# A four-place ring for the first layer's expert weights, filled at the first and second scatter of the following expert

## The chip, the cores and the metric

The kernel runs on one core of one Trainium2 chip. The metric is the device time of one execution in microseconds, as the median of several runs.

## The reference, cut to what matters

A graph network of two layers on 1250 nodes with 512 features. Each layer adds a message-passing part and an attention part to its input and then a mixture of experts. The change touches the experts of the first layer alone:

```python
# first layer, on x = layernorm(...), 1250 x 512
gate_probs = softmax(x @ gate_w.T)                 # 16 experts
top_v, top_i = top_k(gate_probs, 4); top_v = softmax(top_v)
for e in range(16):
    routed += combine[:, e:e+1] * (gelu(x @ re_w1[e] + re_b1[e]) @ re_w2[e] + re_b2[e])   # 512 -> 256 -> 512
shared = mean of two experts that every node goes through
x = x + routed + shared
```

The second layer has 16 experts of another form (two of 16 for a node, 512 to 768 to 512, gated). All arithmetic is in float32.

## The kernel before, in words

The program is a sequence of stages, each a block in which SP (SyncE, which asks for the plain transfers), POOL (GpSimd), PE (TensorE), ACT (ScalarE) and DVE (VectorE) run their own streams and meet at the end. `stage_experts` (line 1084) calls two of them for each layer. `stage_front` computes the gate and the two shared experts, ranks the nodes of each expert (`find_places`) and writes one row for each node to the tensor `token_rows` in HBM. `stage_routed` (line 2012) then goes through the routed experts.

`stage_routed` works in tiles of 128 rows. The rows of one expert fill whole tiles, so an expert has two to four tiles here, and there are 48 tiles in the first layer. For tile g:

- POOL gathers the 128 rows of a tile by an indirect DMA (line 2110, from `token_rows`, two tiles ahead of their use);
- PE turns them (line 2178), DVE copies them (2325, 2326), PE multiplies by the expert's w1 (2194), DVE adds b1 (2332), ACT applies the gelu (2288), PE turns the result (2204), ACT copies it (2280), and PE multiplies by w2 (2214);
- ACT scales the result by the rows' weights (`weigh`, line 2294), and POOL adds it to the rows of `token_sums` in HBM by an accumulating indirect DMA (`add_rows`, line 2119). This is called the scatter of the tile below.

POOL does its part in the order of `tile` (line 2123): copy the scatter's row numbers (`know_add`, 2102) once the scatter two tiles before has landed, since that scatter used the same buffers; issue a gather (2110); wait for the gather before it and copy the next gather's row numbers (2098); wait for earlier scatters; issue the scatter (2119). ACT's `weigh` of a tile waits for `know_add` of it. Two experts can send results to the same node, and an accumulating write is not safe against another to the same row. So the scatter of an expert's first tile waits until all scatters of earlier experts have landed (`landed_by`, lines 2124 and 2138). Scatters of one expert touch different rows and may overlap.

**The ring.** The weights of an expert (w1 512 KB, b1 spread over 128 partitions 128 KB, w2 512 KB) lie in one place of a ring of `RING_EXPERTS` = 3 places at the end of the on-chip arena. Expert e has place e mod 3 (counted from the end). `load_expert` (line 1037) asks for them on SP's queue: w1 (line 1044) and b1 (1045), then w2 (1049). `stage_front` loads the first `early` = 3 experts. In `stage_routed` SP goes through e = 3 to 15 (line 2073): it waits until PE has finished the last w2 product of expert e-3, whose place this is (`down_ready`, which counts PE's tiles; `done_by` holds the number of tiles up to and with an expert, plus one), asks for w1 and b1, then waits until POOL has begun the scatter of the first tile of expert e-2 (`add_begun`, counted just ahead of each scatter), and asks for w2. After the weights of experts 7, 9, 11 and 13 it also asks for 1 MB each of the next stage's attention weights (`MIX_AT`; line 378).

In the second layer the ring has 3 places too, and w2 has no wait of its own.

`find_places` (line 1396, on DVE) derives the place of each tile's expert, `ring_of`, by taking the number of places off again and again, in 5 rounds of two linked operations (lines 1444 to 1448).

Of the kernel before, what the change touches and what calls it, by code (L numbers as in the profile page):

```python
# [25 lines left out]
P = 128  # L26
NODES = 1250
TS = 125
NT = NODES // TS
D = 512  # L30
# [19 lines left out]
ROW = D + NE  # L50
RING_EXPERTS = 3
AHEAD = 4
# [963 lines left out]
class L0_EXPERTS:  # L1016

    top, shared, shared_weight, swiglu = 4, 2, 0.5, False
    slots, early = P, 3
    ff, blocks, w1_cols = 256, 2, 256  # L1020
# [5 lines left out]
class L1_EXPERTS:  # L1026

    top, shared, shared_weight, swiglu = 2, 1, 1.0, True
    slots, early = P, 1
    ff, blocks, w1_cols = 384, 3, 768  # L1030
# [6 lines left out]
def load_expert(sp, rt, kind, ins, e, between=lambda: None):  # L1037

    if e:
        sp.wait_ge(rt.w1_loaded, 32 * e)
    w1, w2, b1 = rt.slot_parts(rt.ring[:, RING_EXPERTS - 1 - e % RING_EXPERTS, :])
    sp.dma_start(w1, ins[kind.w1][e].rearrange("(k p) n -> p k n", p=P)).then_inc(rt.w1_loaded, 16)  # L1044
    sp.dma_start(b1, ins[kind.b1][e].unsqueeze(0).to_broadcast([P, kind.w1_cols])).then_inc(rt.w1_loaded, 16)
    if e:
        sp.wait_ge(rt.w2_loaded, 16 * e)
    between()
    sp.dma_start(w2, ins[kind.w2][e].rearrange("(f p) n -> p f n", p=P)).then_inc(rt.w2_loaded, 16)
# [34 lines left out]
def stage_experts(nc, st, ar, kind, ins, kept, fi, out=None, mw=None, free=None):  # L1084
# [8 lines left out]
    SLOT = KT * W + F * D + W  # L1093
    rt.ring = ar.whole[:, ar.end - RING_EXPERTS * SLOT:ar.end].rearrange("p (r n) -> p r n", r=RING_EXPERTS)
    rt.slot_parts = lambda slot: (slot[:, 0:KT * W].rearrange("p (k n) -> p k n", k=KT),
# [24 lines left out]

    stage_routed(nc, st, SplitArena(ar.whole, free or [(DYN, DYN + KT * NODES + NT * D), (ar.at, ar.end - RING_EXPERTS * SLOT)]),
                 kind, ins, rt, out, mw)


def stage_front(nc, st, ar, kind, ins, rt, fi):
# [62 lines left out]
    with ExitStack() as ctx:  # L1188
# [207 lines left out]
        def find_places(dve):  # L1396
# [46 lines left out]
            link(dve.tensor_copy(rt.expert_of, expert_f))  # L1443
            for r in range(RING_EXPERTS, NE, RING_EXPERTS):
                link(dve.tensor_scalar(lap, expert_f, RING_EXPERTS - 0.5, -float(RING_EXPERTS), ALU.is_gt, ALU.mult))
                link(dve.tensor_tensor(expert_f, expert_f, lap, ALU.add))
            link(dve.tensor_scalar(expert_f, expert_f, -1.0, RING_EXPERTS - 1.0, ALU.mult, ALU.add))
            link(dve.tensor_copy(rt.ring_of, expert_f))
# [563 lines left out]
def stage_routed(nc, st, ar, kind, ins, rt, out, mw):  # L2012
# [4 lines left out]
    F, W, SW = kind.blocks, kind.w1_cols, kind.swiglu  # L2017
    R = RING_EXPERTS
    TILES = 2 * rt.most_pairs
# [23 lines left out]
    with ExitStack() as ctx:  # L2043
# [27 lines left out]
        @block.sync  # L2071
        def _(sp):
            for e in range(kind.early, NE):
                if e >= R:
                    done = sp.value_load(rt.done_by[0:1, e - R:e - R + 1], min_val=1, max_val=TILES + 1)
                    sp.wait_ge(down_ready, done)
                if e >= R and not SW:

                    load_expert(sp, rt, kind, ins, e, lambda: sp.wait_ge(add_begun, done))
                else:  # L2080
                    load_expert(sp, rt, kind, ins, e)
                if mw is not None and e in MIX_AT:
                    mw.load(sp, MIX_AT[e])
            sp.wait_ge(w1_loaded, 32 * NE)
            sp.wait_ge(w2_loaded, 16 * NE)
            sp.wait_ge(all_added, 1)
            if out is None:
                for h, (t0, t1) in enumerate(HALVES):
                    load_tiles(sp, st.res3, sums[1:NODES + 1, :], t0, t1, sums_read[h])
                sp.wait_ge(sums_read[0], 32)  # L2090
                sp.wait_ge(sums_read[1], 32)
# [412 lines left out]
```

## Time and profile before

| | |
|---|---|
| median of 3 runs | 2342.08 us (2335.74, 2342.08, 2342.43) |
| the profiled execution's own time | 2335.63 us |
| its span | 2333.8 us |
| granted TensorE clock, mean | 0.979 |
| PE busy | 2161.1 us, 93% of the span |
| DVE, ACT, POOL busy | 1004.2, 507.6, 309.7 us |
| first to last scatter of the first layer | 842.0 to 1072.3 us, 48 scatters |

Times in the trace are microseconds from the span's start. The span is the time from the first to the last instruction. The profiled execution is the one from which all rows below come. A row of the timeline gives start, duration, engine, line, operation and operands, and in square brackets the idle time of the engine ahead of it with what ended that time. SPq rows are requests for transfers: their duration is that of the request, not of the transfer. An indirect DMA on POOL has the time POOL needs to issue it; the transfer goes on after it. The scatters are numbered here from 0, as they come: scatter 0 is at 842.01.

### The profile page before, as it was taken

What the parts mean: (1) busy time and instruction counts of PE and PEld (TensorE: products, weight loads), DVE (VectorE), ACT (ScalarE), POOL (GpSimd) and SP (SyncE); (2) the same over time, 40 slices, a digit from 0 to 9 for tenths busy, and PEclk for the clock granted to TensorE, in tenths of its full rate; (3) what the DMA queues carried; (4) which work ended last, traced back from release to release, by engine and by line L of the source; (5) the groups of instructions that cost most, each with busy time, mean ns of one, the idle gap of its engine ahead of it and who ended that gap; (6) DMA issues with size and microseconds to landing.
All of it is one profiled execution on the core that took longest, in us unless ns stands there. A gap on an engine that the chain in (4) does not pass through costs nothing. (4 is left out here: it accounts for less than half of the span.)

```text
span 2333.8 us, 26804 instructions
## 1 busy us (share of the span) xinstructions
PE 2161.1 (93%) x7344; PEld 1242.2 (53%) x7345; DVE 1004.2 (43%) x2731; ACT 507.6 (22%) x903; POOL 309.7 (13%) x393
## 2 busy tenths in 40 slices
PE   6998889999998989885999999999899999989997
PEld 3444444545355445554544378854488854545553
DVE  7966778401114622222043465412265413634443
ACT  2112131110103012223111154211244212201221
POOL 1200000000000046562300000000000010013443
PEclk9999999999999999998999999999999999999998
DMA  4003000000002258885000000010100002248773
GB/s 127 1 0 119 1 1 18 1 18 0 0 0 96 90 121 201 222 197 104 36 0 27 25 12 1 1 63 0 37 1 1 1 5 70 80 154 269 216 240 95
DMA packets 77202, 154.58 MB, mean 66 GB/s; under 512 B 10217, under 2 KB 21524, under 8 KB 77116
## 3 DMA queue, kind: packets, MB, share of 16 engines
q1 hardware_dynamic: 59452, 113.06, 14.7%
q0 software_dynamic: 17664, 40.43, 8.7%
q8 instruction: 47, 0.77, 0.1%
q14 instruction: 39, 0.32, 0.0%
HBM read 119.50 MB, written 36.18 MB: 67 GB/s over the span
## 5 line engine op out<-in xcount | busy, mean ns | idle before, releaser
L1918 PE MATMUL bank<-arena 125*125 125x257 f32 x1600 | 355.8, 383 | 4.8 <-DVE arena L1837 4.8
L1918 PEld LDWEIGHTS bank<-arena 125*125 125x125 f32 x1600 | 302.2, 189 | 60.5 <-DVE arena L1837 6.4
L2194 PE MATMUL bank<-arena 128*128 x832 | 258.9, 446 | 13.4 <-issue 6.6
L973 PE MATMUL bank<-arena 125*128 125x500 f32 (+1 forms) x720 | 253.5, 513 | 3.1 <-ACT arena L1002 2.3
L473 PE MATMUL bank<-arena 128*125 128x512 f32 x480 | 212.6, 592 | 2.2 <-PEq L319 2.2
L2194 PEld LDWEIGHTS bank<-arena 128*128 128x128 f32 x832 | 152.0, 193 | 109.7 <-issue 60.0
L1712 PE MATMUL bank<-arena 128*125 128x512 f32 x480 | 207.8, 593 | 1.0 <-PEq L409 1.0
L973 PEld LDWEIGHTS bank<-arena 125*128 125x128 f32 x720 | 135.5, 189 | 121.1 <-issue 109.7
L2214 PE MATMUL bank<-arena 128*128 x360 | 171.2, 604 | 6.2 <-ACT arena L2280 4.0
L2332 DVE TENSOR_TENSOR arena<-bank,arena 128x384 f32<-128x384 f32 (+1 forms) x104 | 51.7, 497 | 257.1 <-PE bank L2194 211.6
L1896 ACT ACTIVATE arena<-arena 125x625 f32<-125x625 f32 x160 | 134.5, 900 | 102.4 <-DVE arena L1837 102.2
L1712 PEld LDWEIGHTS bank<-arena 128*125 128x125 f32 x480 | 89.4, 188 | 113.0 <-issue 112.8
L473 PEld LDWEIGHTS bank<-arena 128*125 128x125 f32 x480 | 86.7, 187 | 101.2 <-issue 101.2
L1837 DVE SCALAR_TENSOR_TENSOR arena<-arena 125x625 f32<-125x625 f32 x160 | 132.4, 864 | 15.6 <-ACT arena L1896 15.6
L735 DVE TENSOR_SCALAR arena<-arena 125x500 bf16<-125x500 f16 x432 | 117.2, 345 | 36.5 <-PE bank L777 36.3
L1768 DVE CUSTOM_DVE_ANT_0 arena<-arena 125x256 f32<-125x256 f32 x160 | 58.2, 422 | 161.5 <-ACT arena L1755 134.7
L913 DVE TENSOR_TENSOR arena<-bank,arena 128x500 f32<-128x500 f32 (+1 forms) x36 | 21.3, 592 | 244.1 <-PE bank L973 244.1
L777 PE MATMUL bank<-arena 125*125 125x500 bf16 x432 | 106.8, 381 | 18.3 <-DVE arena L735 18.2
L2110 POOL DMA_INDIRECT arena<-token_rows,arena x76 | 80.1, 1053 | 163.9 <-DVE arena L2326 129.4
L2214 PEld LDWEIGHTS bank<-arena 128*128 128x128 f32 x360 | 61.6, 191 | 63.0 <-issue 62.0
L777 PEld LDWEIGHTS bank<-arena 125*125 x432 | 57.9, 135 | 69.3 <-issue 52.7
L960 PE MATMUL bank<-arena 128*125 128x512 f32 x184 | 84.0, 619 | 10.5 <-DVE arena L891 9.4
(336 smaller groups left out, 2277.4 us busy)
## 6 DMA issues: line engine op xcount, KB each, us to landing
arena<-in_L_ffn_expert_w SPq DMA_DIRECT2D x16, 1536.0 KB
arena<-in_L_ffn_re_w SPq DMA_DIRECT2D x32, 512.0 KB
arena<-in_L_ffn_expert_w SPq DMA_DIRECT2D x16, 768.0 KB
arena<-in_L_mix_Wqkv SPq DMA_DIRECT2D x6, 1024.0 KB, 10.8
arena<-in_L_gnn_W SPq DMA_DIRECT2D x3, 2048.0 KB, 8.1
arena<-in_L_ffn_expert_b SPq DMA_DIRECT2D x16, 384.0 KB
token_rows<-arena SPq DMA_DIRECT2D x2, 2500.0 KB
arena<-in_L_gnn_W SPq DMA_DIRECT2D x3, 1024.0 KB, 5.5
```

The lines of the kernel that those rows point to most:

```text
L473: last = pe.matmul(st.bank[n % 4][0:TS, :], st.turned[:, k, t * TS:(t + 1) * TS], w3[:, k, j * D:(j + 1) * D], start=(k == 0), stop=(k == ...
L735: last = dve.tensor_scalar(marks[:, u, :], st.iota16[:, 0:WIN * NT], float(w * WIN * NT), keys[:, u:u + 1], ALU.add, ALU.is_equal)
L777: last = pe.matmul(bank, stays[:, u, :], marks[:, u, :], start=False, stop=False, skip_group_check=True)
L960: last = pe.matmul(st.bank[s % 4][0:TS, :], X[:, k, s * TS:(s + 1) * TS], w[:, k, :], start=(k == 0), stop=(k == KT - 1))
L973: last = pe.matmul(st.bank[4 + n % 4][:, 0:cn], h[s][:, f * P:(f + 1) * P], st.counts[:, s, c0:c0 + cn], start=(s == 0), stop=(s == NT - 1))
L1712: last = pe.matmul(st.bank[n % 4][0:TS, :], x, w[:, half * 512:(half + 1) * 512], start=(k == 0), stop=(k == K - 1))
L1837: dve.scalar_tensor_tensor(out=prob[:, u % 2, s, :], in0=excess[:, n % EXCESS, :], scalar=by_one[:, s, head:head + 1], in1=st.counts16[:, ...
L1896: act.activation(excess[:, n % EXCESS, :], row[:, head, d0:d0 + HALF], ACT.Relu, scale=by_fifth[:, s, head:head + 1], bias=minus_one[:, s, ...
L1918: return pe.matmul(st.bank[n % OUTS][0:TS, 0:ONCOL], prob[:, u % 2, s, j * TS:(j + 1) * TS], st.slots[:, head + 1, s, :], start=(s == 0), ...
L2110: pool.indirect_dma_start(out=rows[b], out_offset=None, in_=rt.table, in_offset=bass.IndirectOffsetOnAxis(ap=get_row[b].bitcast(mybir.dt.u ...
L2194: last = pe.matmul(st.bank[UP[b][h]][:, 0:WP], xt[b][:, k, :], rt.ring[:, bass.ds(r, 1), k * W + h * WP:k * W + (h + 1) * WP].rearrange("p ...
L2214: last = pe.matmul(st.bank[DOWN[b]], ht[b][:, f, :], rt.ring[:, bass.ds(r, 1), W2_AT + f * D:W2_AT + (f + 1) * D].rearrange("p a n -> p (a ...
```

## The change

The number of places becomes a property of the layer: 4 in the first, 3 in the second. In the first layer SP's wait for a place changes with it. Expert e now takes the place of expert e-4. w1 and b1 are asked for when POOL has begun the scatter of the first tile of expert e-3, the one that follows the place's owner, and w2 at the scatter after that. The second layer's rule stays (`down_ready`). The four attention loads still follow the w2 request of their expert.

```diff
-RING_EXPERTS = 3
 ...
 class L0_EXPERTS:
-    slots, early = P, 3
+    slots, early, ring = P, 3, 4
 class L1_EXPERTS:
-    slots, early = P, 1
+    slots, early, ring = P, 1, 3
 ...
 def load_expert(sp, rt, kind, ins, e, between=lambda: None):
-    w1, w2, b1 = rt.slot_parts(rt.ring[:, RING_EXPERTS - 1 - e % RING_EXPERTS, :])
+    w1, w2, b1 = rt.slot_parts(rt.ring[:, kind.ring - 1 - e % kind.ring, :])
 ...
-            for r in range(RING_EXPERTS, NE, RING_EXPERTS):
-                link(dve.tensor_scalar(lap, expert_f, RING_EXPERTS - 0.5, -float(RING_EXPERTS), ALU.is_gt, ALU.mult))
+            for r in range(kind.ring, NE, kind.ring):
+                link(dve.tensor_scalar(lap, expert_f, kind.ring - 0.5, -float(kind.ring), ALU.is_gt, ALU.mult))
                 link(dve.tensor_tensor(expert_f, expert_f, lap, ALU.add))
 ...
-    R = RING_EXPERTS
+    R = kind.ring
 ...
             for e in range(kind.early, NE):
                 if e >= R:
                     done = sp.value_load(rt.done_by[0:1, e - R:e - R + 1], min_val=1, max_val=TILES + 1)
-                    sp.wait_ge(down_ready, done)
+                    sp.wait_ge(down_ready if SW else add_begun, done)
                 if e >= R and not SW:
-                    load_expert(sp, rt, kind, ins, e, lambda: sp.wait_ge(add_begun, done))
+                    load_expert(sp, rt, kind, ins, e, lambda: sp.wait_ge(add_begun, done + 1))
                 else:
                     load_expert(sp, rt, kind, ins, e)
```

How the instructions stand on the engines is shown at two places. A name in a bracket is that of a semaphore; semaphores are reused, so `step_49` is here `down_ready` and `ident_ready_49` is `add_begun`. `re_w` stands for w1 (line 1044, in the changed kernel 1043) and w2 (1049, then 1048), `re_b` for b1.

SP before, at the start of `stage_routed` of the first layer: the loads of experts 3 and 4.

```order
L2071 UNCONDITIONAL_BRANCH [waits barrier_Pool_Activation_PE_DVE_SP_release]
L2075 TENSOR_LOAD arena
L2075 ISA x2
L1044 DMA arena<-in_L_ffn_re_w 128x4x256 [waits w1_loaded_4,step_49]
L1045 DMA arena<-in_L_ffn_re_b 128x256
L1049 DMA arena<-in_L_ffn_re_w 128x2x512 [waits ident_ready_49,w2_loaded_4]
L2075 TENSOR_LOAD arena
L2075 ISA x2
L1044 DMA arena<-in_L_ffn_re_w 128x4x256 [waits w1_loaded_4,step_49]
L1045 DMA arena<-in_L_ffn_re_b 128x256
L1049 DMA arena<-in_L_ffn_re_w 128x2x512 [waits ident_ready_49,w2_loaded_4]
```

SP with the change, at the same place.

```order
L2070 UNCONDITIONAL_BRANCH [waits barrier_Pool_Activation_PE_DVE_SP_release]
L1043 DMA arena<-in_L_ffn_re_w 128x4x256 [waits w1_loaded_4]
L1044 DMA arena<-in_L_ffn_re_b 128x256
L1048 DMA arena<-in_L_ffn_re_w 128x2x512 [waits w2_loaded_4]
L2074 TENSOR_LOAD arena
L2074 ISA x2
L1043 DMA arena<-in_L_ffn_re_w 128x4x256 [waits w1_loaded_4,ident_ready_49]
L1044 DMA arena<-in_L_ffn_re_b 128x256
L2079 REGISTER_ALU [waits w2_loaded_4]
L1048 DMA arena<-in_L_ffn_re_w 128x2x512 [waits ident_ready_49]
```

Expert 3 is loaded at once, with no wait for a tile; from expert 4 on both parts wait for scatters, and neither for PE.

DVE in `find_places` with the change (first layer). Before, lines 1445 and 1446 (now 1444 and 1445) stood there five times each.

```order
L1442 CAST arena<-arena 125x56
L1444 TENSOR_SCALAR arena<-arena 125x56
L1445 TENSOR_TENSOR arena<-arena 125x56
L1444 TENSOR_SCALAR arena<-arena 125x56
L1445 TENSOR_TENSOR arena<-arena 125x56
L1444 TENSOR_SCALAR arena<-arena 125x56
L1445 TENSOR_TENSOR arena<-arena 125x56
L1446 TENSOR_SCALAR arena<-arena 125x56
```

Two of five rounds are gone, four operations in all.

## Rows read from the trace of the kernel before

**Rows 1.** Line 2119 in the window 842 to 1075: count, issue time, first and last start.

```profile
L2119 POOL DMA_INDIRECT token_sums<-arena x48: 1591/1598/1626, 842.0 to 1072.3; - x48
```

**Rows 2.** Stretches: width, busy PE, PEld, DVE, ACT, POOL; clock, DMA share, GB/s.

```profile
920.00:1027.00 107.00, 95.08 (x382) 56.37 (x381) 25.03 (x64) 29.99 (x64) 62.90 (x84) 1.00 0.89 222
...
1037.00:1065.00 28.00, 26.24 (x106) 16.02 (x106) 6.32 (x16) 8.75 (x18) 17.99 (x24) 1.00 0.73 130
```

**Rows 3.** Timeline of POOL, scatters 3, 12, 13, 14, 15 and 16, and one copy.

```profile
858.93 1.60 POOL L2119 DMA_INDIRECT token_sums<-arena  x1 [1.42 <-DMA token_sums<-arena]
...
899.56 1.60 POOL L2119 DMA_INDIRECT token_sums<-arena  x1 [0.53 <-issue]
906.70 1.60 POOL L2119 DMA_INDIRECT token_sums<-arena  x1 [1.81 <-DMA token_sums<-arena]
...
910.25 1.60 POOL L2119 DMA_INDIRECT token_sums<-arena  x1 [0.31 <-issue]
911.79 0.26 POOL L2102 COPY arena<-arena 128x1 int32 x1
...
914.35 1.60 POOL L2119 DMA_INDIRECT token_sums<-arena  x1 [0.44 <-issue]
...
920.26 1.60 POOL L2119 DMA_INDIRECT token_sums<-arena  x1 [1.09 <-issue]
```

**Rows 4.** The same timeline: a copy and the scatters 18, 19, 25, 31.

```profile
928.87 0.18 POOL L2102 COPY arena<-arena 128x1 int32 x1 [3.18 <-DMA token_sums<-arena]
...
931.03 1.60 POOL L2119 DMA_INDIRECT token_sums<-arena  x1 [0.17 <-issue]
...
936.63 1.60 POOL L2119 DMA_INDIRECT token_sums<-arena  x1 [2.17 <-DMA token_sums<-arena]
...
966.47 1.60 POOL L2119 DMA_INDIRECT token_sums<-arena  x1 [2.19 <-DMA token_sums<-arena]
...
996.79 1.60 POOL L2119 DMA_INDIRECT token_sums<-arena  x1 [2.23 <-DMA token_sums<-arena]
```

**Rows 5.** The same timeline: scatter 37, a copy, scatters 39 and 45.

```profile
1027.13 1.60 POOL L2119 DMA_INDIRECT token_sums<-arena  x1 [2.17 <-DMA token_sums<-arena]
...
1033.21 0.23 POOL L2102 COPY arena<-arena 128x1 int32 x1
...
1037.50 1.60 POOL L2119 DMA_INDIRECT token_sums<-arena  x1 [1.93 <-DMA token_sums<-arena]
...
1065.09 1.60 POOL L2119 DMA_INDIRECT token_sums<-arena  x1 [1.61 <-DMA token_sums<-arena]
```

**Rows 6.** Timeline of SP's requests around scatters 13 to 16, and by scatter 37.

```profile
906.00 0.37 SPq L1049 DMA_DIRECT2D arena<-in_L_ffn_re_w  x1
911.91 0.37 SPq L1044 DMA_DIRECT2D arena<-in_L_ffn_re_w  x1
...
919.57 0.37 SPq L1049 DMA_DIRECT2D arena<-in_L_ffn_re_w  x1
919.98 0.46 SPq L378 DMA_DIRECT2D arena<-in_L_mix_Wqkv  x1
...
1028.32 0.37 SPq L1044 DMA_DIRECT2D arena<-in_L_ffn_re_w  x1
```

**Rows 7.** Waits in the window 842 to 1072: who for whom, us, times, longest.

```profile
PE bank L2214 <- DMA arena<-in_L_ffn_re_w: 1.0, 2, 0.7
```

**Rows 8.** The attention weights' three loads 920 to 980, time to landing.

```profile
DMA to landing us min/median/max: 7.1/8.1/8.4
```

**Rows 9.** Timelines: the start of `stage_routed`, POOL's gather and PE's second turn.

```profile
829.45 0.98 POOL L2145 DMA_INDIRECT arena<-token_rows,arena  x1 [0.57 <-POOL arena L2142]
...
837.97 0.60 PE L2178 MATMUL bank<-arena 128*128 128x128 f32 x4
```

**Rows 10.** Timelines of DVE and PE in `stage_front`: a ring round, the wait behind.

```profile
786.62 0.22 DVE L1446 TENSOR_TENSOR arena<-arena 125x56 f32<-125x56 f32 x1
...
795.89 3.68 PE L1332 MATMUL bank<-arena 128*125 128x512 f32 x8 [0.17 <-DVE arena L1600]
```

More of the change, by code:

```diff
@@ L1093, in stage_experts @@
     SLOT = KT * W + F * D + W
-    rt.ring = ar.whole[:, ar.end - RING_EXPERTS * SLOT:ar.end].rearrange("p (r n) -> p r n", r=RING_EXPERTS)
+    rt.ring = ar.whole[:, ar.end - kind.ring * SLOT:ar.end].rearrange("p (r n) -> p r n", r=kind.ring)
     rt.slot_parts = lambda slot: (slot[:, 0:KT * W].rearrange("p (k n) -> p k n", k=KT),
@@ L1119, in stage_experts @@
     stage_front(nc, st, Arena(ar.whole, ar.at, ar.end - kind.early * SLOT), kind, ins, rt, fi)
-    stage_routed(nc, st, SplitArena(ar.whole, free or [(DYN, DYN + KT * NODES + NT * D), (ar.at, ar.end - RING_EXPERTS * SLOT)]),
+    stage_routed(nc, st, SplitArena(ar.whole, free or [(DYN, DYN + KT * NODES + NT * D), (ar.at, ar.end - kind.ring * SLOT)]),
                  kind, ins, rt, out, mw)
@@ L1443, in find_places @@
             link(dve.tensor_copy(rt.expert_of, expert_f))
-            for r in range(RING_EXPERTS, NE, RING_EXPERTS):
-                link(dve.tensor_scalar(lap, expert_f, RING_EXPERTS - 0.5, -float(RING_EXPERTS), ALU.is_gt, ALU.mult))
+            for r in range(kind.ring, NE, kind.ring):
+                link(dve.tensor_scalar(lap, expert_f, kind.ring - 0.5, -float(kind.ring), ALU.is_gt, ALU.mult))
                 link(dve.tensor_tensor(expert_f, expert_f, lap, ALU.add))
-            link(dve.tensor_scalar(expert_f, expert_f, -1.0, RING_EXPERTS - 1.0, ALU.mult, ALU.add))
+            link(dve.tensor_scalar(expert_f, expert_f, -1.0, kind.ring - 1.0, ALU.mult, ALU.add))
             link(dve.tensor_copy(rt.ring_of, expert_f))
```

## The prediction

> **What bounds the kernel now.** The change touches one stage, the routed experts of the first layer, so I went from the page to the stretch in which this stage's scatters run: 48 of them, from 842.0 to 1072.3 [rows 1]. The table of stretches comes first. While weights are loaded (920 to 1027) PE is busy for 95.08 of 107 us (89%), and the DMA engines for 0.89 of the time; once nearly all are in (1037 to 1065), PE is busy for 26.24 of 28 us (94%) and the DMA share is 0.73 [rows 2]. PE does not wait for the weights themselves: its products with w2 stand behind that weight's transfer for 1.0 us in the whole stage [rows 7]. So something that the weight traffic slows stands between.
>
> The timeline of POOL shows what. Take three experts: tiles 10 to 12, 13 to 15, and 16 to 18. The first tile's scatter of an expert must find all earlier scatters landed, and it does wait: scatter 13 comes 7.14 us after scatter 12, scatter 16 comes 5.91 after 15, scatter 19 comes 5.60 after 18 [rows 3, 4]. I call this time the **boundary**. The other half of the period is the time from an expert's first to its last scatter, the **inside**. There the last tile's row copy has to wait for the first tile's scatter to land, since both use the same buffers: scatter 15 comes 7.65 after 13, but scatter 18 comes 10.77 after 16 [rows 3, 4]. So a period holds two landings in series, that of the first tile's scatter and that of the last tile's. The middle tile's landing is not in this chain unless it is over 2 us late. In a stretch with almost no loads, six tiles take 27.59 us, 13.8 for three [rows 5]; with loads and attention weights six tiles take 29.93 (13 to 19), 29.84 (19 to 25), 30.32 (25 to 31) and 30.34 (31 to 37) [rows 3 to 5].
>
> SP's rows say which load stands beside which landing. A w2 is asked for 0.70 us before an expert's first scatter (906.00, 919.57), a w1 with its b1 2.44 us before its last (911.91 before 914.35), and 1 MB of attention weights 0.28 us before a first scatter (919.98) [rows 3, 6]. The two bad cases follow. Where w1 stands beside the last scatter, the boundary is 5.91 to 7.14 us, against 5.60 with none (18 to 19). Where the attention weights stand beside the first scatter, its landing is late and the copy behind it comes at 928.87, 8.61 us after the scatter; without them it comes at 911.79, 5.09 us after [rows 3, 4].
>
> **The change, part by part.** Times are of the profiled execution, 2335.63 us, whose span is 2333.8.
>
> *w1 leaves the last scatter.* After the change w1 goes out 0.7 us before an expert's first scatter, w2 0.7 before its second, and nothing near the last one. So a boundary should be 5.60.
>
> *w1 stands beside the first scatter.* There w2 stood before, and the copy came 5.09 us later, when POOL was free for it, so w2 cost nothing there. How w1 with b1 does is not seen alone. Lower bound: as w2, nothing. Upper bound: scatter 37, which has a w2 (0.70 before) and a w1 (asked for at 1028.32, 1.19 after) beside it; its copy comes after 6.08 us, 1.0 later than the 5.09 [rows 5, 6]. w1 with b1 is 640 KB against 1152 KB there and 512 KB of w2, so I take nearer to the lower end: 0.4. The inside becomes 8.05, a period without attention weights 8.05 + 5.60 = 13.65. The stretch almost without loads ran at 13.8, part of it limited by PE's own pace; I take 13.7.
>
> Ten tiles, scatters 3 to 13, took 47.77 [rows 3]. At 13.7 for three tiles they take 45.7, and the four-tile expert among them has only one boundary for four tiles, some 0.5 less: 45.2. **Gain 2.6.**
>
> *The attention weights move.* They follow a w2, so they now go out right ahead of a middle scatter. Its late landing is off the chain: the middle comes 3.6 after the first (906.70 to 910.25), its copy 8.6 later, and a next first scatter 2.2 behind the copy (928.87 to 931.03), which is 14.4, less than the period below. What they still do is slow the last scatter, 4.5 us behind. Lower bound: nothing, a boundary of 5.60. Upper bound: w2, attention weights and the w1 ahead of them fill the DMA engines past the last scatter; the worst boundary in rows 3 and 4 is 7.14, and I put the bound at 8.0 (estimate). I take 7.0, near the 7.14 that a w1 beside the last scatter gave. The period is 8.05 + 7.0 = 15.05, and with its partner without attention weights 13.7 + 15.05 = 28.75. Four such pairs take 115.0, against 120.43 from scatter 13 to 37 [rows 3, 5]. **Gain 5.4.**
>
> *The ends.* Scatters 37 to 39 (10.37 us) have w1 and w2 beside them before and after; from 39 on there is next to nothing: 0. At the start, expert 3 is now loaded at once (1152 KB), beside the first gathers; the one issued at 829.45 is turned by PE at 837.97, and 8 us cover a delay of a few [rows 9]. If that cover were gone the cost would be 1 to 2 us. The w1 that stood beside the first tiles goes, and there scatters wait for one another anyway: 0.
>
> *DVE.* Four linked operations of 0.22 us, some 0.9 us, go from `stage_front`. PE waits behind them only 0.17 [rows 10], so **0.2** at most.
>
> *SP and PE.* SP's queue is idle between requests, and an added register instruction costs nothing there. Weights arrive three tiles sooner; with PE's waits for w2 at 1.0 us in all [rows 7] (and those I read as the last of several causes), I count 0. The second layer is as before.
>
> Sum: 2.6 + 5.4 + 0.2 = 8.2 us, so 2327.4 for the profiled execution. The median of the three runs is 2342.08, 6.4 above it, so the prediction is **2333.9**. What comes next as the bound is PE, at the pace of the last stretch.
>
> The Trainium skill ("DMA: Bandwidth & Descriptors", section "Queues, rings and completion order") says that a transfer's completion count is written only after every earlier write of that DMA engine, across its queues. It speaks against this change, since w1 would then hold the first scatter's landing until its own data is down; the trace agrees as far as that with 1 MB ahead, which takes 8.1 us to land [rows 8], the scatter's copy comes 8.61 us later. By it the sum would be that of the first rival.
>
> **Rivals.**
>
> 1. *The burden only changes place.* The first scatter lands only when w1 and b1 have, some 6 us after it is begun, as with scatter 37 (6.08) [rows 5]. Each inside grows by 1.0, not 0.4. For it: the mix-laden scatter's landing follows that of the 1 MB. Against it: w2 in the same place costs nothing. Price: 0.6 more in about 11 periods, 6.6 of the 8.2 go back: 2340.5, no difference. The point: a copy 6 us after the first scatter.
>
> 2. *Slower: the two sets pile up.* w1 and w2 are now 3.6 us apart and not 5.9 or 7.7 [rows 3, 6]. If the engines are not done with one when the next and two gathers come, first and last scatter are late together. The DMA share is already 0.89 [rows 2]. Price: a copy after 7.0 us, between 6.08 and the 8.61 of the mix, makes the inside 9.6, a period 15.2, and one with attention weights 9.6 + 7.0 = 16.6. Ten tiles take 15.2 x 10/3 = 50.7 (2.9 lost), four pairs 127.2 (6.8 lost): 9.7 slower, 2351.8. It decides from where an average period of 14.3 (47.77 x 3/10) is passed: a copy later than 6.2 us. Against it: nothing is then asked for from the second scatter to the next first, which lets the engines catch up.
>
> 3. *It does not do what it says.* SP asks in order, and each request also waits until the previous expert's has landed. Were that late, w1 would slip from the first scatter to a later one. Against it: before, w2 went out at 906.00 and the next w1 at 911.91, with time between [rows 6]. Then about 2342.
>
> **How the numbers follow.** My forecast has 0.62, rival 1 has 0.21, rival 2 0.12, rival 3 0.05. The measurement can tell about 0.3%, 7.0 us. The forecast's own bounds: at best 8.2 + 0.4 x 11 + 1.4 x 4 = 18.2, but the last stretch's pace (27.59 / 6 = 4.60 a tile) leaves 13.0 (scatters 3 to 39: 36 tiles at 4.60 are 165.6, against 178.6), so 13 and 1 for a PE a little faster still; at worst 8.2 - 0.6 x 11 - 1.0 x 4, 2.4 slower. Within it 0.44 lies beyond 7.0 and 0.18 inside. Rival 1 gives 0.19 to no change and 0.02 to slower, rival 2 its 0.12 to slower, rival 3 its 0.05 to no change. Together 0.44, 0.42, 0.14. The runs before lie at 2335.74 and at 2342, so the lower end is 2335.7 less 14, and the upper end 2342.4 plus 3.5.
>
> **What would show it.** Right: w1 0.7 us before each first scatter from scatter 3 on; boundaries of 5.6 in all experts without attention weights; insides of about 8; pairs at 28.75; the time from scatter 3 to 39 some 8 us under 178.6. Wrong: row copies of last tiles more than 6 us after the first scatter, boundaries of over 7 with nothing beside them, or PE waiting for gathers with the chain of scatters already short.

## The result, and the profile after

The change makes the kernel slower, by 0.6%: 2352.94 us median (2349.47 to 2354.31, 4 runs) against 2340.63 (2335.74 to 2342.43, 4 runs); ratio 1.0059, 95% interval 1.0046 to 1.0071. The profiled execution took 2354.31 us with a span of 2352.5, 18.7 more than the span before. That is more than the 12.3 between the medians, since the profiled execution before (2335.63) lies at the lower end of its runs and this one is the slowest of its four. The forecast was 2333.9, faster, with a range of 2322 to 2346.

First the scatters as a whole, as in [rows 1], in the changed kernel:

```profile
L2119 POOL DMA_INDIRECT token_sums<-arena x48: 1591/1598/1626, 844.7 to 1091.6; - x48
```

From first to last scatter it takes 246.9 us and not 230.3. The first scatter comes 2.7 us later, and 0.6 comes back behind the last. The stretches of the routed stage, before and then after (columns as in [rows 2]):

```profile
842.00:1072.00 230.00, 206.85 (x832) 123.57 (x831) 53.40 (x136) 66.93 (x141) 140.72 (x187) 1.00 0.84 193
```

```profile
844.00:1092.00 248.00, 216.35 (x842) 127.66 (x840) 53.38 (x136) 68.42 (x143) 141.51 (x190) 0.97 0.77 175
```

The DMA engines are less busy after the change (0.77, before 0.84), PE too. So the loss is not more work for them on average; something waits. The granted TensorE clock is 0.97 of 2.4 GHz, 1.00 before, so for some 6% of this stretch (an estimate, if it was at 2.4 GHz for the rest) PE was at the lower level, 1.2 GHz, and that goes with longer waits of PE behind gathers (below). It is part of why PE's busy time is 216.35 and not 206.85. It is not where the loss starts: from 860 to 880, where the first expert below falls, the granted clock is 1.00, and experiment 7 has 0.97 from 860 to 1060 as the changed kernel has, and is still shorter by 10.7 us. The clock is lowest from 940 to 960 (0.85), behind a stretch in which PE was busy for 16.0 of 20 us.

Where it waits is in the timeline of POOL. (SP's lines have moved up by one: 1043 asks for w1, 1044 for b1, 1048 for w2. In the experiments POOL's lines shift by a few too; names and order are the same.) Here are the scatters 3, 4, 5 and 6, an expert of three tiles without attention weights, after the change:

```profile
861.53 1.60 POOL L2119 DMA_INDIRECT token_sums<-arena  x1 [1.56 <-DMA token_sums<-arena]
862.79 0.54 POOL L2102 COPY arena<-arena 128x1 int32 x1
863.57 1.01 POOL L2110 DMA_INDIRECT arena<-token_rows,arena  x1 [0.25 <-issue]
864.59 0.20 POOL L2098 COPY arena<-arena 128x1 int32 x1
865.08 1.60 POOL L2119 DMA_INDIRECT token_sums<-arena  x1 [0.29 <-issue]
867.11 0.18 POOL L2102 COPY arena<-arena 128x1 int32 x1 [0.43 <-DMA token_sums<-arena]
868.03 1.01 POOL L2110 DMA_INDIRECT arena<-token_rows,arena  x1 [0.74 <-issue]
870.93 0.18 POOL L2098 COPY arena<-arena 128x1 int32 x1 [1.89 <-DMA arena<-token_rows,arena]
871.89 1.60 POOL L2119 DMA_INDIRECT token_sums<-arena  x1 [0.78 <-DMA token_sums<-arena]
...
877.56 1.60 POOL L2119 DMA_INDIRECT token_sums<-arena  x1 [2.32 <-issue]
```

and SP's requests beside them:

```profile
860.79 0.38 SPq L1043 DMA_DIRECT2D arena<-in_L_ffn_re_w  x1
861.21 0.51 SPq L1044 DMA_DIRECT2D arena<-in_L_ffn_re_b  x1
864.34 0.37 SPq L1048 DMA_DIRECT2D arena<-in_L_ffn_re_w  x1
```

Read it line by line. SP asks as intended: w1 0.74 us ahead of the first scatter, w2 0.74 ahead of the second. The first scatter lands in time: its copy comes 5.58 us after it (867.11). The boundary is 5.67 (871.89 to 877.56), where 5.60 was expected. But the copy of line 2098 at 870.93 stood for 1.89 us behind a gather, the one issued at 863.57, **between the expert's first and second scatter** and 0.77 us ahead of the w2 request. POOL sees it landed after 7.4 us (the trace's own time from issue to landing is 7.2). The last scatter is queued behind that copy, and so comes 10.36 us after the first; in the same expert before it came 7.84 after (858.93 to 866.77). The sum is 2.04 to the gather, 7.36 to the copy, and 0.96 from the copy to the scatter. That last part was 0.36 in the same expert before the change, where the copy ran without a wait; in 11 of the 12 places where the changed kernel's copy waited it is 0.89 to 0.96. So a waited copy costs some 0.6 us more than its wait; why is not shown. Before, in the expert of tiles 13 to 15, the same place reads:

```profile
908.73 1.01 POOL L2110 DMA_INDIRECT arena<-token_rows,arena  x1 [0.23 <-issue]
...
912.70 1.01 POOL L2110 DMA_INDIRECT arena<-token_rows,arena  x1 [0.65 <-issue]
913.72 0.19 POOL L2098 COPY arena<-arena 128x1 int32 x1
```

4.99 us after the gather's issue the copy that needs it (913.72) runs with no wait. I call this gather the **middle gather** below. In all three-tile experts without attention weights the copy comes 5.6 to 7.4 us after the middle gather in the changed kernel, and 4.7 to 5.4 before, there without a wait.

With attention weights behind w2 (tiles 13 to 15) it is worse, after the change:

```profile
911.16 1.60 POOL L2119 DMA_INDIRECT token_sums<-arena  x1 [1.99 <-DMA token_sums<-arena]
...
913.19 1.01 POOL L2110 DMA_INDIRECT arena<-token_rows,arena  x1 [0.23 <-issue]
...
916.98 0.18 POOL L2102 COPY arena<-arena 128x1 int32 x1 [0.67 <-DMA token_sums<-arena]
...
921.40 0.18 POOL L2098 COPY arena<-arena 128x1 int32 x1 [2.51 <-DMA arena<-token_rows,arena]
922.35 1.60 POOL L2119 DMA_INDIRECT token_sums<-arena  x1 [0.77 <-issue]
...
928.92 1.60 POOL L2119 DMA_INDIRECT token_sums<-arena  x1 [1.64 <-issue]
```

The middle gather takes 8.2 us to be seen landed, the inside is 11.19. The waits over the whole stage say the same; after the change:

```profile
POOL arena L2098 <- DMA arena<-token_rows,arena: 22.7, 12, 3.5
...
PE bank L2178 <- DMA arena<-token_rows,arena: 17.4, 12, 2.6
```

Before, the first of these waits does not occur, and PE's is:

```profile
PE bank L2178 <- DMA arena<-token_rows,arena: 4.3, 5, 1.8
```

The sums by stretch, scatter to scatter, are in the table at the end of the next section.

### The profile page after: what moved, and what is told of

Its sections match the earlier page's. It is cut to its first block and busy times, and to the rows that moved or that the text cites. A ratio compares the mean times of both kernels' runs of the same rounds, so it can differ in the third digit from the quotient of the medians.

```text
span 2352.5 us, 26795 instructions
## 1 busy us (share of the span) xinstructions
PE 2173.1 (92%) x7344; PEld 1248.3 (53%) x7345; DVE 1003.3 (43%) x2727; ACT 508.0 (22%) x903; POOL 309.3 (13%) x393
## 5 line engine op out<-in xcount | busy, mean ns | idle before, releaser
L2194 PE MATMUL bank<-arena 128*128 x832 | 261.8, 451 | 13.7 <-issue 4.0
L2214 PE MATMUL bank<-arena 128*128 x360 | 176.6, 620 | 5.8 <-ACT arena L2280 5.6
L959 PE MATMUL bank<-arena 128*125 128x512 f32 x184 | 84.1, 620 | 10.5 <-DVE arena L890 9.4
```

The costliest lines, as they stand in the source:

```text
L959: last = pe.matmul(st.bank[s % 4][0:TS, :], X[:, k, s * TS:(s + 1) * TS], w[:, k, :], start=(k == 0), stop=(k == KT - 1))
L2194: last = pe.matmul(st.bank[UP[b][h]][:, 0:WP], xt[b][:, k, :], rt.ring[:, bass.ds(r, 1), k * W + h * WP:k * W + (h + 1) * WP].rearrange("p ...
L2214: last = pe.matmul(st.bank[DOWN[b]], ht[b][:, f, :], rt.ring[:, bass.ds(r, 1), W2_AT + f * D:W2_AT + (f + 1) * D].rearrange("p a n -> p (a ...
```

## The experiments

Each ratio below is to runs of the kernel before from the same batch (medians 2336.75, 2337.38 and 2337.86 us). The times from scatter to scatter are from one profiled execution of each kernel. Kernel 1, whose requests are timed as before, differs by 2.5 us from scatter 3 to 39, so differences of that size say little.

Two theories at the start, from this profile. The **gather theory**: the last scatter is held by the middle gather, which is late because a set is asked for just behind it. The **pile-up theory**: the two sets of an expert are too close together (3.6 us), wherever they lie. Beside them: the attention weights' new place is the whole loss, or the fourth place itself is.

**1. The fourth place alone.** The ring has four places, the waits are those of before.

```diff
-                if e >= R:
-                    done = sp.value_load(rt.done_by[0:1, e - R:e - R + 1], ...)
-                    sp.wait_ge(down_ready if SW else add_begun, done)
+                if e >= 3:
+                    done = sp.value_load(rt.done_by[0:1, e - 3:e - 2], ...)
+                    sp.wait_ge(down_ready, done)
...
-                    load_expert(..., lambda: sp.wait_ge(add_begun, done + 1))
+                    load_expert(..., lambda: sp.wait_ge(add_begun, done))
```

> Four places, but the waits of before: w1 when PE has finished the last tile of expert e-3, w2 at the first scatter of expert e-2, expert 3 too. Theory A (the loss comes from when the sets are asked for): as the kernel before, within 0.3%; scatters 3 to 39 in 178 to 180 us (before 178.6, changed 195.2). Rival (the fourth place itself costs, by where it lies in the arena or by the shorter ring search on DVE): 5 us or more slower than before.

Measured: ratio 1.0003 (0.9992 to 1.0013), scatters 3 to 39 in 181.1 us. That is 1.1 over the 178 to 180 I gave, but 14 under the changed kernel. The place and the shorter search on DVE cost nothing that a run can tell. Its first scatter comes at 845.3:

```profile
L2119 POOL DMA_INDIRECT token_sums<-arena x48: 1592/1598/1626, 845.3 to 1079.2; - x48
```

So the later start of the changed kernel (844.7, before 842.0) need not come from expert 3's early load; this kernel has it without that load, and so has number 8 (844.5), whose requests are those of before.

**2. Both sets at the first scatter.** w2 has no wait of its own.

```diff
-                if e >= R and not SW:
-                    load_expert(..., lambda: sp.wait_ge(add_begun, done + 1))
-                else:
-                    load_expert(sp, rt, kind, ins, e)
+                load_expert(sp, rt, kind, ins, e)
```

> Four places, w1 and w2 both asked for at the first scatter of expert e-3, w2 with no wait of its own. Gather theory (what ends the time from an expert's first to its last scatter is the landing of the gather issued between the first and the second scatter, and it is late when a set is asked for just behind that gather): the sets are ahead of the gather, which lands 5.5 to 6 us after it is asked for and not 7 to 8; scatters 3 to 13 in 45 to 48 us (changed 49.6). Pile-up theory (the two sets lie too close together): they are now 0 us apart and not 3.6, so it is worse than the change, scatters 3 to 13 in 51 us or more. The attention weights are then asked for at first scatters again, ahead of which both sets lie: 10 us and more from first to last scatter there under both theories.

Measured: ratio 1.009 (1.0069 to 1.0112), scatters 3 to 13 in 53.0 us. With attention weights the insides are 11.4 to 12.3, as both theories said. The gather theory's 45 to 48 was wrong, the pile-up theory's number right. The same expert in the timeline of POOL shows another wait than the change's, though:

```profile
863.52 1.60 POOL L2114 DMA_INDIRECT token_sums<-arena  x1 [1.54 <-DMA token_sums<-arena]
...
871.54 0.18 POOL L2097 COPY arena<-arena 128x1 int32 x1 [2.87 <-DMA token_sums<-arena]
...
873.48 0.19 POOL L2093 COPY arena<-arena 128x1 int32 x1
873.84 1.60 POOL L2114 DMA_INDIRECT token_sums<-arena  x1 [0.17 <-issue]
```

With 1152 KB ahead of it the first scatter itself is late: its copy comes after 8.02 us (5.58 with w1 and b1 alone), and by then the gather has landed, so the copy at 873.48 waits for nothing. Whatever is late first, the inside is over 10 us. This run does not speak for either theory in the change; it adds the price of a second set beside the first scatter.

**3. Only w2 moved.** w1 stays where it was, beside the last scatter; w2 and the attention weights go to the second scatter.

```diff
 # against experiment 1
-                    load_expert(..., lambda: sp.wait_ge(add_begun, done))
+                    load_expert(..., lambda: sp.wait_ge(add_begun, done + 1))
```

> Four places, w1 as before (when PE has finished the last tile of expert e-3), only w2 and the attention weights behind it moved to an expert's second scatter. Gather theory: w2 goes out just behind the gather between first and second scatter, so that gather is late (6 to 8 us) although no w1 is near; from first to last scatter 9 us or more without attention weights, 10.5 or more with them; the loss of the change remains in large part: 8 to 18 us slower than before. Pile-up theory: the sets are 6 us or more apart, so no loss, within 0.3% of before.

Measured: ratio 1.0095 (1.0075 to 1.0115), 3 to 39 in 198.0 us. That is some 22 us slower, over the 8 to 18 that I gave and more than the change itself. Nothing of the pile-up theory's "no loss" came. In the first expert w2 is asked for just ahead of the second scatter, and no w1 is near until 2.4 us later:

```profile
862.95 0.37 SPq L1048 DMA_DIRECT2D arena<-in_L_ffn_re_w  x1
865.34 0.39 SPq L1043 DMA_DIRECT2D arena<-in_L_ffn_re_w  x1
```

```profile
862.18 1.01 POOL L2109 DMA_INDIRECT arena<-token_rows,arena  x1 [0.25 <-issue]
...
868.83 0.18 POOL L2097 COPY arena<-arena 128x1 int32 x1 [1.66 <-DMA arena<-token_rows,arena]
869.79 1.60 POOL L2118 DMA_INDIRECT token_sums<-arena  x1 [0.77 <-DMA token_sums<-arena]
```

The middle gather's copy comes after 6.65 us, the inside is 9.66. The next w1 follows this w2 after 2.4 us, and in the other three-tile experts after 2.4 to 3.3, so "6 us or more apart", as I wrote for the rival, does not hold there. It holds in the expert of four tiles that comes next: w2 is asked for at 878.12, the w1 before it went out 12.8 us earlier (865.34), the one behind it 8.1 us later.

```profile
877.88 1.01 POOL L2109 DMA_INDIRECT arena<-token_rows,arena  x1 [0.65 <-issue]
...
883.97 0.18 POOL L2097 COPY arena<-arena 128x1 int32 x1 [1.65 <-DMA arena<-token_rows,arena]
884.87 1.60 POOL L2118 DMA_INDIRECT token_sums<-arena  x1 [0.72 <-DMA token_sums<-arena]
```

w2 alone, 0.24 us behind the gather: the copy comes after 6.1 us and the third scatter 9.44 after the first (875.43), where in the same expert before they came after 4.7, without a wait, and 7.64 (872.91 to 880.55). So this run does tell the theories apart: no second set is needed. My 10.5 or more with attention weights did not come in all: those four insides are 8.9, 9.5, 10.5 and 11.2, while their boundaries grew to 8.0 to 8.5 (5.6 to 5.8 in the others). Number 5 asks the same with w1.

**4. The change without attention weights in the loop.** All four are asked for after expert 15's weights.

```diff
-                if mw is not None and e in MIX_AT:
-                    mw.load(sp, MIX_AT[e])
+            if mw is not None:
+                mw.load(sp)
             sp.wait_ge(w1_loaded, 32 * NE)
```

> The change, but all four parts of the attention weights are asked for together after expert 15's weights. Theory that the attention weights' new place beside the second scatter is nearly the whole loss: scatters 3 to 39 in 168 to 174 us (changed 195.2, before 178.6), from first to last scatter 8 us. Gather theory: w2 alone delays the gather too, from first to last scatter 9 to 10 us in all three-tile experts, scatters 3 to 39 in 178 to 184 us. Pile-up theory: the same 178 to 184.

Measured: ratio 1.0058 (1.0037 to 1.0079), scatters 3 to 39 in 189.0 us. The attention weights are not the whole loss: without them this stretch is still 10.4 us longer than before, which carried them. The insides are 9.3 to 11.0 in three-tile experts. It is more than the 178 to 184 of the gather theory, since 9 to 10 was my guess for all, and the 4 MB fall together beside scatter 38 (the boundary to 39 is 9.82). In the whole time nothing is regained (1.0058, the change 1.0059): the 4 MB also make the stretch from scatter 39 to the last 38.1 us long, against 34.9.

**5. Only w1 moved.** w2 stays at the first scatter as before; w1 goes from the last tile to the second scatter.

```diff
 # against the change
-                    sp.wait_ge(down_ready if SW else add_begun, done)
...
-                    load_expert(..., lambda: sp.wait_ge(add_begun, done + 1))
+                    if SW:
+                        sp.wait_ge(down_ready, done)
+                        load_expert(sp, rt, kind, ins, e)
+                    else:
+                        then = sp.value_load(rt.done_by[0:1, e - 3:e - 2], ...)
+                        sp.wait_ge(add_begun, done + 1)
+                        load_expert(..., lambda: sp.wait_ge(add_begun, then))
```

> Four places; w1 and b1 of expert e at the second scatter of expert e-3, w2 at the first scatter of expert e-2, as before. So against the kernel before only w1 is moved, from 2.4 us ahead of the last scatter to just ahead of the second. Gather theory: the gather between first and second scatter is late as with w2 there, 6 to 7.5 us, so 9.2 us or more from first to last scatter; 6 to 15 us slower than before. Pile-up theory: w1 and w2 are further apart than in the change (3.6 and 10 us), most of the loss is gone: within 3 us of before. If nothing near the last scatter is what matters: boundaries of 5.6, and faster than before by 5 us.

Measured: ratio 1.0052 (1.0036 to 1.0069), 3 to 39 in 189.0 us, 0.5% slower, as the gather theory said. In the expert of scatters 3 to 5 w1 with b1 is the only set, the next w2 comes 11.3 us later:

```profile
866.40 0.38 SPq L1043 DMA_DIRECT2D arena<-in_L_ffn_re_w  x1
866.83 0.50 SPq L1044 DMA_DIRECT2D arena<-in_L_ffn_re_b  x1
877.69 0.37 SPq L1048 DMA_DIRECT2D arena<-in_L_ffn_re_w  x1
```

```profile
865.63 1.01 POOL L2112 DMA_INDIRECT arena<-token_rows,arena  x1 [0.25 <-issue]
...
871.75 0.18 POOL L2100 COPY arena<-arena 128x1 int32 x1 [1.13 <-DMA arena<-token_rows,arena]
```

6.1 us from the gather to the copy that waited for it, an inside of 9.12, with one set in sight. In the same expert before it was 5.4 us without a wait, and an inside of 7.84. Pile-up is not needed for this 1.3 us. From the next expert on a w2 lies some 3.4 us ahead of w1, and in those without attention weights the copy comes after 6.4 to 6.9 us. Boundaries are 5.4 to 5.7 with nothing beside the last scatter; that gain is real and too small.

**6. w2 2.8 us later.** As the change, but w2 waits until POOL begins the gather that follows the second scatter (`gather_begun`, counted ahead of each gather).

```diff
-                    load_expert(..., lambda: sp.wait_ge(add_begun, done + 1))
+                    load_expert(..., lambda: sp.wait_ge(gather_begun, done + 2))
```

> The change, but w2 (and the attention weights behind it) waits until POOL begins the gather that follows an expert's second scatter, some 2.4 us after that scatter. Gather theory: the gather between first and second scatter then lands in 4.5 to 5.5 us and not 6 to 8, the last scatter comes 7.7 to 8.6 us after the first; what w2 then costs shows in the last scatter's landing (5.6 to 6.6 us to the next first scatter, with attention weights 7.5 to 8.5). Scatters 3 to 13 in 46 to 48.5 us (changed 49.6), 3 to 39 in 178 to 188 (changed 195.2). If it is w1 beside the first scatter that makes that gather late, nothing is regained: 193 us or more.

Measured: ratio 1.0016 (1.0007 to 1.0026), 3 to 13 in 46.4, 3 to 39 in 184.7 us. Both times are within what the gather theory gave. Not within it are insides of 8.7 and 9.0, a boundary of 6.9 without attention weights, and boundaries of 9.2 to 9.8 with them (7.5 to 8.5 expected). The expert of scatters 3 to 5, POOL and then SP:

```profile
861.98 1.01 POOL L2110 DMA_INDIRECT arena<-token_rows,arena  x1 [0.24 <-issue]
...
867.35 0.19 POOL L2098 COPY arena<-arena 128x1 int32 x1
867.71 1.60 POOL L2119 DMA_INDIRECT token_sums<-arena  x1 [0.17 <-issue]
```

```profile
865.60 0.38 SPq L1048 DMA_DIRECT2D arena<-in_L_ffn_re_w  x1
```

The copy waits for nothing, the last scatter comes 7.77 us after the first (859.94). w1 is beside the first scatter as in the change, so w1 by itself does not make the gather late.

**7. The wait taken out of the way.** The requests are those of the change. In the first layer POOL issues a tile's scatter before it waits for the gather and copies the next row numbers.

```diff
-                if not last:
+                if SW and not last:
                     pool.wait_ge(rows_loaded[1 - b], i * 16 + 48)
                     know_get(g + 1, 1 - b)
                 for odd in range(2):
                     pool.wait_ge(landed[odd], earlier[odd])
                 add_rows(g, b)
+                if not SW and not last:
+                    pool.wait_ge(rows_loaded[1 - b], i * 16 + 48)
+                    know_get(g + 1, 1 - b)
```

> The change, requests untouched; in the first layer POOL issues a tile's scatter first and only then waits for the gather issued a tile before and copies the next gather's row numbers. Gather theory (that wait, standing ahead of the last scatter, turns the late gather into a longer period): the last scatter comes 8 to 8.6 us after the first where there are no attention weights (changed 9 to 10.4), scatters 3 to 13 in 45 to 47.5 us, 3 to 39 in 180 to 188 (changed 195.2). PE, which needs the same gather, may then wait for it. Theory that PE's need of the late rows is the bound by itself, or the engines are full: no gain, 3 to 39 in 193 or more.

Measured: ratio 1.0026 (1.0012 to 1.0041), 3 to 39 in 184.5 us, insides 7.8 to 8.9 (two of them over the 8.6 that I gave). With SP's requests in the places of the change, 10.7 of the 16.6 us come back. In the expert of scatters 3 to 5 the last scatter no longer stands behind the copy:

```profile
868.13 1.60 POOL L2119 DMA_INDIRECT token_sums<-arena  x1 [0.30 <-issue]
869.33 0.61 POOL L2098 COPY arena<-arena 128x1 int32 x1
```

The gather is still late, and PE does wait for it, more than before the change (4.3 us) and less than in it (17.4):

```profile
PE bank L2181 <- DMA arena<-token_rows,arena: 11.8, 7, 2.7
```

but the period no longer hangs on it. What is left lies in the boundaries behind the attention weights, 8.65 to 10.48 us (in the change 6.55 to 6.57).

**8. The same order in the kernel before.**

The edit is that of experiment 7, made to the kernel before.

> The kernel before (three places, its waits) with the scatter ahead of the wait for the gather in the first layer. Its gathers between first and second scatter land in 4.1 to 4.6 us and are not waited for long, so by the gather theory next to nothing: 0 to 3 us faster, scatters 3 to 39 in 176 to 178.6. If the wait mattered as much before, 5 us or more.

Measured: ratio 0.9998 (0.9988 to 1.0008), 3 to 39 in 177.4 us. The wait was idle before, as its rows show. So it was the change that made it matter.

**9. Attention weights at the start of the stage, waits of before.** On top of experiment 1:

```diff
+            if mw is not None:
+                mw.load(sp)
             for e in range(kind.early, NE):
...
-                if mw is not None and e in MIX_AT:
-                    mw.load(sp, MIX_AT[e])
```

> Four places with the waits of before, and the 4 MB of attention weights asked for at the start of the stage, ahead of expert 3, so none beside a scatter later. Theory that in the kernel before it is the attention weights beside a first scatter that make four of the experts 3 us longer: from first to last scatter 7.6 to 8.1 us in all three-tile experts, scatters 3 to 39 in 164 to 170 us (before 178.6). At the start the first gathers and scatters wait for 4 MB (some 20 us of transfers), 3 to 10 us lost there; in all 2 to 10 us faster than before. Rival (the DMA engines as a whole are the bound, and the work only moves): no change within 0.3%.

Measured: ratio 0.9989 (0.9979 to 0.9999), 3 to 39 in 172.2 us, 6.4 under before and 2 over the range I gave. The insides are 7.4 to 8.4, so the attention weights beside a first scatter were what made four of them 3 us longer. In the whole time some 2.6 us are left (0.9989): 1.6 of the 6.4 go at the start (first scatter at 843.6, before 842.0), less than the 3 to 10 that I expected, and 1.0 behind scatter 39. That is within my 2 to 10 us, but also within the rival's 0.3%; it is the scatters' times that speak against the rival.

**10. Both: w2 at the gather, attention weights at the start.**

The edits of experiments 6 and 9 on the changed kernel.

> As the first of these (change, w2 at the gather that follows the second scatter), with the attention weights at the start of the stage. Gather theory: from first to last scatter about 8 us, to the next first 5.6 to 6.4; scatters 3 to 39 in 166 to 172 us. If w1 beside the first scatter makes the gather late: 178 us or more. The start as in the run before.

Measured: 2328.19 us median, ratio 0.9959 (0.9945 to 0.9973): faster than both kernels. Scatters 3 to 39 take 169.6 us; first to last:

```profile
L2119 POOL DMA_INDIRECT token_sums<-arena x48: 1592/1599/1627, 845.7 to 1068.4; - x48
```

222.7 us, 7.6 under before. 5.1 MB are asked for at once at the start (DMA share 0.89 in 826 to 846; columns as in [rows 2]). The first scatter is later than before, but it comes at 845.3 in number 1 as well, so that the 5.1 MB delay it is not shown:

```profile
826.00:846.00 20.00, 13.44 (x47) 9.63 (x47) 3.79 (x9) 2.27 (x5) 4.13 (x9) 0.66 0.89 304
```

**11. That kernel with the scatter ahead of the wait.**

The edit of experiment 7 on top of experiment 10.

> The fastest so far (w2 at the gather that follows the second scatter, attention weights at the start of the stage), with the scatter ahead of the wait for the gather in the first layer. There the gathers land in 4 to 5 us and hardly hold a scatter: 0 to 4 us faster than that kernel, scatters 3 to 39 in 165.5 to 169.6. If moving the row-number copy behind the scatter makes the next gather late: slower by 1 to 4.

Measured: ratio 0.9953 (0.9937 to 0.997), 3 to 39 in 169.6 us. No difference from number 10 can be told.

All kernels in one table, in us, from the scatters' starts; insides of three-tile experts, from scatter 3 to 37.

| kernel | 3 to 13 | 13 to 37 | 3 to 39 | insides | ratio |
|---|---|---|---|---|---|
| before | 47.8 | 120.4 | 178.6 | 7.6 to 8.1, with attention weights 10.4 to 10.8 | 1 |
| changed | 49.6 | 134.3 | 195.2 | 8.9 to 10.4, with attention weights 11.2 to 11.8 | 1.0059 |
| 1 fourth place alone | 48.3 | 122.2 | 181.1 | 7.7 to 7.9, 10.1 to 10.9 | 1.0003 |
| 2 both at the first | 53.0 | 133.2 | 197.2 | 9.9 to 10.8, 11.4 to 12.3 | 1.0090 |
| 3 only w2 moved | 50.1 | 134.8 | 198.0 | 8.9 to 11.2 | 1.0095 |
| 4 change, attention last | 49.8 | 124.8 | 189.0 | 9.3 to 11.0 | 1.0058 |
| 5 only w1 moved | 50.0 | 126.7 | 189.0 | 9.1 to 11.9 | 1.0052 |
| 6 w2 at the gather | 46.4 | 127.9 | 184.7 | 7.6 to 9.0 | 1.0016 |
| 7 change, scatter ahead | 47.0 | 126.6 | 184.5 | 7.8 to 8.9 | 1.0026 |
| 8 before, scatter ahead | 46.8 | 119.7 | 177.4 | 7.8, 9.6 to 10.4 | 0.9998 |
| 9 place, attention first | 47.2 | 114.8 | 172.2 | 7.4 to 8.4 | 0.9989 |
| 10 both of 6 and 9 | 45.5 | 113.8 | 169.6 | 7.7 to 9.5 | 0.9959 |
| 11 that, scatter ahead | 45.2 | 113.9 | 169.6 | 7.8 to 8.6 | 0.9953 |

## Why the prediction was wrong

**The step that failed** is "*w1 stands beside the first scatter* ... The inside becomes 8.05". It took the inside to be set by one landing, that of the first tile's scatter. That landing came out about as estimated: the copy behind it comes 5.3 to 6.1 us after the scatter, where I took 5.5. The inside is 8.9 to 10.4 in experts without attention weights, not 8.05. But POOL's stream has a second wait ahead of the last scatter, for the middle gather, and I did not list it, although the order of POOL's steps that I worked from has it (line 2132). Before, it never held POOL, so no row of the waits named it. The middle gather is issued 2.0 us after the first scatter, the new w2 request goes out 2.8 us after it. I asked what w1 and w2 do to scatters and never what the moved w2 does to the gather beside it. Shown by: the wait of 1.89 us in the change; the recovery when w2 goes 2.8 us later (6) and when the wait is moved instead (7), 10.5 and 10.7 of 16.6 us; a late middle gather with w2 alone (3) and with w1 and b1 alone (5) behind it.

**The same gap in "*The attention weights move*".** "Its late landing is off the chain" holds for the middle scatter's landing, although that took 10.4 to 11.0 us and not 8.6, and the boundary came out at 6.57, under the 7.0 I took. But the attention weights made the middle gather later still (8.2 us to its copy), and the period is 11.19 + 6.57 = 17.76 us against 15.05. The partner expert came at 15.97 (scatters 16 to 19) against 13.7. Over the four pairs the forecast was 115.0, measured 134.3: 19.3 of the error, most of it. Three to 13 missed by 4.4 (49.6 against 45.2).

**Half right was** that two landings in series make the period. The boundary is the last scatter's landing. The inside hung on the first scatter's landing where attention weights stood beside it: the copy at 928.87 waited 3.18 us. But the one at 911.79 ran without a wait, so the 7.65 to which I added 0.4 was not set by that landing.

**Right were** that w1 beside the last scatter costs at the boundary (5.55 to 5.82 in all experts without attention weights after the change, as said), that PE's waits for weights are nothing, and that ring and DVE cost nothing (1). The start's 0 is not contradicted, since kernels 1 and 8 start as late.

**The rivals.** Rival 2, the one on the slower side, gave 9.7 us more and was nearest to what was measured (+12.3 between the medians), but its point of decision, a copy later than 6.2 us, never came. Its place was wrong, so its size is no confirmation of it. Its half sentence on "two gathers" held the cause, without a price. Rival 1's point, a copy after 6 us, was reached in one expert of the eleven from scatter 3 to 36 (6.06), and numbers 9 and 10 speak against it: with no attention weights beside scatters, moving w1 from the last scatter to the first makes 3 to 39 not longer (169.6 against 172.2). Rival 3 did not occur: w1 went out 0.74 or 0.75 us ahead of each first scatter from scatter 3 to 37. The rule of the Trainium skill quoted there ("DMA: Bandwidth & Descriptors", "Queues, rings and completion order") was put to the wrong transfer: it speaks as much of a gather as of a scatter. A gather that is seen landed after 7.4 us with 512 KB asked for 0.77 us later agrees with completion being held by other queues' writes, if some of those writes go out ahead of the gather's last, for the rule is of earlier writes. It agrees as well with that section's other rule, engines taking turns between queues; no run here separates the two.

**What is left in numbers 6 and 7.** Both are 6 us longer than before from scatter 3 to 39, and that is nearly all in the four periods with attention weights: they take 71.7 us (6) and 70.2 us (7), against 64.8 before; their partners take 56.2 and 56.4, against 55.7, and scatters 3 to 13 are shorter than before in both. So attention weights behind a middle scatter, where they hold the boundary, cost more than beside a first one, where they hold the inside. Without them beside any scatter (10) nothing is lost.

**What stays open**: what in the DMA engines makes a gather late by a set that is asked for after it, and why the scatter comes 0.6 us later still when the copy ahead of it had to wait.

## What to carry to other kernels

Before a request is moved in time, list every transfer in flight at the new place, the other kind too, and for each the first instruction that waits for it and what is queued behind that instruction. A wait that shows no idle time in the profile has a margin, not a guarantee: compute it. When a stream has to wait for something that only a later step needs, put the work that others wait for ahead of it; it cost nothing where the wait was idle (8) and gave back 10.7 us where it was not (7).

## What the runs showed of the hardware

A transfer asked for *after* a gather can delay it: 640 KB asked for 0.8 us behind it, with no other set near, moved the copy that waits for it from 5.4 us or less to 6.1 (5, the expert of scatters 3 to 5); 512 KB asked for 0.2 us behind a gather, with no other set within 8 us, moved it from 4.7 or less to 6.1 (3, the expert of four tiles). One expert's value is loose: in the expert of scatters 3 to 5, with the same requests beside it, the copy comes after 7.4 us in the change and 6.4 in number 4. 512 KB asked for 3.6 us behind the gather did not delay it beyond 5.4 (6: gather at 861.98, request at 865.60). And the kernel lost time while the DMA engines grew less busy (0.84 to 0.77): here the share alone did not tell when a transfer that something waits for is finished.
